# Hot ids as 4 KB spread by TensorE in a recommendation tower, with a new order of the work

## The chip, the core and the metric

The kernel runs on one NeuronCore of a Trainium2 chip. Its engines work side by side and meet through semaphores: TensorE (PE in the profile, with its weight loads as PEld), VectorE (DVE), ScalarE (ACT), GpSimd (POOL) and SyncE (SP), which only issues loads here. The metric is the device time of one execution in microseconds. Before the change it was 199.67 us, the median of three runs (199.2 to 199.85).

## The reference

For 512 samples, 32 tables give one row of 64 numbers each. Every pair of the 32 rows goes through its own 64 x 64 matrix, and the 496 results plus 16 dense features go through three dense layers:

```python
e = jnp.stack([tbl_0[ids[:, 0]], ..., tbl_31[ids[:, 31]]], axis=1)   # (512, 32, 64)
idx_i, idx_j = np.triu_indices(32, k=1)
left = jnp.einsum('bpd,pde->bpe', e[:, idx_i, :], L0_rec_W)
z = jnp.sum(left * e[:, idx_j, :], axis=-1)                          # (512, 496)
h = jnp.concatenate([z, dense_ctx], axis=1)
h = jnp.maximum(h @ W_top1 + b_top1, 0.0)                            # 512
h = jnp.maximum(h @ W_top2 + b_top2, 0.0)                            # 256
y = h @ W_top3
```

Everything is float32, the ids are int32.

## The kernel before

The samples are cut into 4 parts of 128, one sample per partition. The 32 fields form 16 units of two fields. The 496 pairs are covered by 31 groups; group 0 pairs fields inside the units, groups 1 and 2 and the 28 others pair unit with unit. So there are 31 x 4 = 124 group products. For each, TensorE multiplies the turned rows (`xt`) with the pair weights into `left` in PSUM (three slots), and VectorE multiplies `left` with the other fields and writes 1024 numbers per partition. Then the products are summed in one of four ways, the letter in the order: C, TensorE multiplies with a selector (`reduce`, line 737); A, ScalarE adds them by accumulating copies (`add_rows`, line 442, 16 copies each); D, VectorE itself (`sum_rows`, line 611); P, GpSimd by halving (`add_halves`, line 409).

Rows come by indirect DMA on GpSimd (`fetch`, line 396), one field of 128 samples each. "Turning" a unit means transposing it on TensorE (line 692) and copying it to `xt` by ScalarE (an `a` behind the word) or VectorE.

Eight fields with tables of at most 1024 rows are hot. In part 0 their rows, units 12 to 15, are not gathered: the tables are loaded whole, VectorE compares the ids, which lie broadcast over all partitions, with the row numbers (`compare`, line 515, 16 compares), and TensorE multiplies the tables with these 0/1 matrices (`look_up`, line 675). That makes 24 gathers in part 0 and 32 in each of the other parts, 120 in all. The ids of the first 4 hot fields and those of the other 4 each come as a broadcast of 256 KB; their homes are the last `prod_act` buffer.

The order of everything is written by hand in a table of words, `ORDER`. Every engine walks through all of it and takes what is its own, so an engine waits only where its own next step is not ready. In it `o1.0` is a compare (second set, first half), `h1` a look-up, `0g9` a gather (part 0, unit 9), `0t8-11a` a turn of units 8 to 11 by ScalarE, `0:22A` the product of group 22 of part 0, `0=22` its sum, `u` the way back of the hot rows, `f0` and `z0` the end of a part's sums, `l`, `m` and `n` layers 1 to 3. A group of way C reads its other fields from `xt`, so it needs their turn; one of the other ways reads them from `rows`, so it needs their gather.

SyncE loads the ids, the hot ids and the 8 hot tables (256 KB each), then the 31 pair weights (256 KB each). From the ninth on, each of these loads waits until VectorE has taken the product eight places earlier (`W_AHEAD`). Behind them come the dense features and the MLP weights (line 370, 1.5 MB).

Of the kernel before, what the change touches and what calls it, by code (L numbers as in the profile page):

```python
# [11 lines left out]
I32 = mybir.dt.int32  # L12
# [200 lines left out]
def build(nc, a):  # L213
    ctx = ExitStack()
    with ctx:
# [111 lines left out]
        def summed(part, g):  # L327
            way = WAY[part, g]
            return {"A": act_added, "P": pool_summed, "D": dve_summed, "C": reduce_done}[way], SUMS[way].index((part, g)) + 1

        block = ctx.enter_context(nc.Block())

        @block.sync
# [587 lines left out]
```

## Time and profile before

| | |
|---|---|
| median of the runs | 199.67 us |
| time of the profiled execution | 199.53 us |
| its span, first to last instruction | 197.4 us |
| busy: PE, PEld, DVE, ACT, POOL | 189.4, 156.6, 179.8, 170.4, 144.7 us |
| granted TensorE clock, mean | 1.00 |
| moved by DMA | 16.82 MB |

The profile describes the one profiled execution; times inside it are counted from the start of its span. The ends of matmuls are modelled, so a busy PE can be waiting for its next operands or for a free slot; PEld is the safer measure. In the views an fp32 matmul stands as two entries. Neighbouring instructions of VectorE overlap by about 0.08 us, so that the distance of two starts, not the duration, is what one costs.

### The profile page before, as it was taken

How to read it: one execution, taken by the hardware profiler on the slowest of the kernel's cores; microseconds unless marked ns; L12 is line 12 of the kernel's file. 1: busy time of each engine (PE TensorE's matmuls, PEld its weight loads, DVE VectorE, ACT ScalarE, POOL GpSimd, SP SyncE). 2: the span in 40 equal slices, each digit the busy share in tenths (PEclk: the TensorE clock that was granted, in tenths of full speed). 3: DMA queues.
4: the chain of work that ended last, by engine and by line, in shares of the span. 5: the costliest groups of instructions: out<-in, count | busy, mean ns of one | idle time of the engine just before them, and what ended most of it. 6: DMA issues, size and time to landing. Idle time of an engine off the chain costs nothing.

```text
span 197.4 us, 7040 instructions
## 1 busy us (share of the span) xinstructions
PE 189.4 (96%) x2380; PEld 156.6 (79%) x2380; DVE 179.8 (91%) x188; ACT 170.4 (86%) x1535; POOL 144.7 (73%) x181
## 2 busy tenths in 40 slices
PE   6889989899999999999999999999999999999994
PEld 6878848697758688798688878897687788778993
DVE  4656799999989999999999999999999999999951
ACT  6005979799997999999949999999999999999942
POOL 5787777777777777777777777777777997887810
PEclk9999999999999999999999999999999999999999
DMA  4969978867561111111111111111111000000000
GB/s 146 357 226 345 244 216 246 248 211 209 171 213 27 31 27 30 28 30 27 32 29 27 29 28 25 31 27 30 32 27 27 18 2 5 0 0 7 0 0 3
DMA packets 11100, 16.82 MB, mean 85 GB/s; under 512 B 3624, under 2 KB 3624, under 8 KB 10936
## 3 DMA queue, kind: packets, MB, share of 16 engines
q1 hardware_dynamic: 7224, 12.43, 19.1%
q0 software_dynamic: 3840, 3.94, 10.0%
q8 instruction: 19, 0.31, 0.7%
q14 instruction: 17, 0.14, 0.2%
HBM read 16.36 MB, written 0.00 MB: 83 GB/s over the span
## 4 chain that ended last, share of the span: by engine, by line
PE 66%; POOL 18%; issue 7%; DMA 4%; DVE 3%; ACT 0%; DVEq 0%; ACTq 0%; POOLq 0%
PE left L714 26%; POOL rows L396 18%; PE left L724 14%; PE zsum L737 8%; PE left L787 6%; PE left L797 4%; DMA rows<-tbl_dram,ids 3%; PE left L703 3%; PE left L692 2%; PE zsum L745 1%; DVE prod_act L566 1%; PE left L781 1%; PE left L772 1%; DMA ids<-ids_dram 1%; DVE sums L611 1%
## 5 line engine op out<-in xcount | busy, mean ns | idle before, releaser
L442 ACT ACTIVATE prod_act<-prod_act 128x64 f32<-128x64 f32 x752 | 157.7, 588 | 2.5 <-DVE prod_act L566 2.5
L442 ACT ACTIVATION_READ_ACCUMULATOR prod_act<-prod_act 128x1 f32 x752 | 155.5, 501 | 0.0
L396 POOL DMA_INDIRECT rows<-tbl_dram,ids x120 | 114.8, 957 | 37.5 <-issue 32.6
L714 PE MATMUL left<-w,xt 64*128 64x256 f32 (+1 forms) x600 | 72.0, 378 | 1.0 <-DVE prod_act L566 0.9
L714 PEld LDWEIGHTS left<-w,xt 64*128 64x128 f32 x600 | 52.5, 187 | 12.5 <-issue 4.1
L566 DVE TENSOR_TENSOR prod_act<-left,rows 128x1024 f32<-128x1024 f32 x47 | 56.3, 1213 | 5.5 <-PE left L714 3.6
L586 DVE TENSOR_TENSOR prod_col<-left,xt 128x1024 f32<-128x1024 f32 x43 | 50.7, 1214 | 0.7 <-PE left L724 0.2
L724 PEld LDWEIGHTS left<-xt,w 64*128 64x128 f32 x768 | 46.5, 188 | 3.5 <-DVE prod_act L566 1.1
L724 PE MATMUL left<-xt,w 64*128 64x128 f32 x768 | 48.7, 275 | 0.2 <-DVE prod_act L566 0.2
L409 POOL TENSOR_TENSOR prod_pool<-prod_pool 128x512 f32<-128x512 f32 (+4 forms) x45 | 27.3, 608 | 4.9 <-DVE prod_pool L560 1.0
L737 PE MATMUL zsum<-prod_col,selector 128*32 128x256 f32 x384 | 24.6, 384 | 0.0
L611 DVE TENSOR_REDUCE sums<-prod_dve 128x16 f32<-128x1024 f32 x20 | 23.7, 1207 | 0.0
L566 DVE TENSOR_TENSOR prod_dve<-left,rows 128x1024 f32<-128x1024 f32 x16 | 19.2, 1213 | 0.1
L737 PEld LDWEIGHTS zsum<-prod_col,selector 128*32 128x32 f32 x384 | 10.6, 109 | 8.7 <-issue 1.7
L479 ACT ACTIVATE xt<-left 128x512 f32<-128x512 f32 (+5 forms) x12 | 9.1, 771 | 5.7 <-PE left L692 5.7
L787 PE MATMUL left<-z,w 128*128 128x256 f32 (+1 forms) x64 | 12.1, 337 | 0.0
L787 PEld LDWEIGHTS left<-z,w 128*128 128x128 f32 x64 | 9.6, 190 | 2.6 <-DVE prod_act L566 0.8
L471 ACT ACTIVATE xt<-left 128x256 f32<-128x256 f32 x1 | 0.4, 385 | 11.1 <-PE left L675 11.1
L515 DVE TENSOR_SCALAR prod_col<-prod_act,row_cast 128x512 f32<-128x512 int32 x16 | 6.5, 480 | 2.9 <-DMA prod_act<-hot_ids_dram 2.9
L692 PEld LDWEIGHTS left<-ident,rows 64*128 64x128 f32 x120 | 5.2, 138 | 4.5 <-issue 2.3
L703 PE MATMUL left<-w,xt 64*128 64x64 f32 x128 | 7.8, 271 | 0.0
L797 PE MATMUL left<-h,w 128*128 128x128 f32 (+1 forms) x48 | 7.6, 312 | 0.0
(52 smaller groups left out, 110.0 us busy)
## 6 DMA issues: line engine op xcount, KB each, us to landing
w<-pair_w_dram SPq DMA_DIRECT2D x31, 256.0 KB, 3.7
rows<-tbl_dram,ids POOLq DMA_INDIRECT x120, 2.5
w<-tbl_dram SPq DMA_DIRECT2D x6, 256.0 KB, 4.9
w<-w_top_dram SPq DMA_DIRECT2D x1, 1024.0 KB
prod_act<-hot_ids_dram SPq DMA_DIRECT2D x2, 256.0 KB, 4.0
h<-tbl_dram SPq DMA_DIRECT2D x2, 256.0 KB, 6.2
w<-w_top_dram SPq DMA_DIRECT2D x1, 512.0 KB
z<-dense_t_dram SPq DMA_DIRECT2D x16, 2.0 KB
```

Source lines behind the costliest of these rows:

```text
L396: pool.indirect_dma_start(out=rows[:, part % ROW_BUFS, n, h, :], out_offset=None, in_=a[f"tbl_{f}"], in_offset=bass.IndirectOffsetOnAxis(a ...
L409: pool.tensor_tensor(prod[:, :, :half], prod[:, :, :half], prod[:, :, half:2 * half], ALU.add).then_inc(pool_halved, 1)
L442: op = act.activation(p, p, ACT.Copy, accum_out=act_sums[:, k:k + 1])
L566: dve.tensor_tensor(out.rearrange("p (j e) d -> p j (e d)", j=4), slot(item).rearrange("p (j e) -> p j e", j=4), other.unsqueeze(1).to_bro ...
L586: dve.tensor_tensor(out.rearrange("p h (j m) b -> p (h j) (m b)", j=2), slot(item).rearrange("p (j e) -> p j e", j=4), other, ALU.mult).th ...
L611: dve.tensor_reduce(sums_of(part, g), prod.rearrange("p (h u o) d -> p h u o d", h=2, o=2), AXIS.X, ALU.add).then_inc(dve_summed, 1)
L703: mm = pe.matmul(slot(item)[:, col:col + D], xt[own, part % 2, 2 * k + half, :], w[own, INSIDE, :, :].rearrange("p u c -> p (u c)")[:, D * ...
L714: mm = pe.matmul(slot(item)[:, col:col + P * per], xt[own, part % 2, GROUPS[g][i][0], :], w[own, g, i:i + per, :], start=True, stop=True)
L724: mm = pe.matmul(slot(item)[:, col:col + PB], w[own, g, i, :], xt[own, part % 2, n, :], start=True, stop=True)
L737: mm = pe.matmul(zsums(pair)[32 * s:32 * s + 32, :], selector[:, 30 - 2 * q:62 - 2 * q], prod_col[:, (COL_FROM + c) % COL_BUFS, half, odd: ...
L787: mm = pe.matmul(slot(item)[:, :n], w1[:, c, P * k:P * k + P], z[:, c, SPANS[i]], start=(c == 0), stop=(c == NZ - 1))
L797: mm = pe.matmul(slot(item)[:, BANK * o:BANK * o + n], w2[:, k, P * o:P * o + P], h1[:, k, :n], start=(k == 0), stop=(k == H1 // P - 1))
```

## The change

It has two parts. The first is how the hot ids of part 0 reach all partitions. They come as 8 x 128 integers (4 KB) into the first 8 partitions of a `prod_dve` buffer; VectorE casts them to float; for each set of four fields TensorE multiplies them with a column of the identity matrix, broadcast, so that each field's ids appear on all 128 partitions in PSUM (`spread`, in `zsum` and `act_sums`, which are not yet in use); ScalarE copies the 512 numbers to where the loads put them before; VectorE compares floats. The warm-up of TensorE falls from 12 matmuls to 3.

The second is a new `ORDER` for the whole kernel. It has the same 124 products and 120 gathers. 49 groups instead of 48 are summed by TensorE, 47 as before by ScalarE, 20 as before by VectorE, 8 instead of 9 by GpSimd. There are 13 turns instead of 15: 9 by ScalarE (12 before) and 4 by VectorE (3 before).

```diff
--- before.py
+++ after.py
@@ ORDER and ACT_GROUPS @@
-    "o0.0 0g9 0g8 o0.1 0g10 o1.0 o1.1 h0 0g10 0g9 0g11 0g8 h1a 0g11 0g4 0:22A 0g6 0g4 0g6 0g5 0:30C 0t8-11a 0:29C",
...
+    "o0.0 0g9 o0.1 0g7 h0a 0g9 o1.0 o1.1 0g7 0g8 0g6 h1 0g6 0g8 0:21A 0:30C 0g4 0:27D 0:28A 0g5 0=21 0g4 0=30 0g5",
...
-ACT_GROUPS = [15, 19, 24, 11, 18, 22, 9, 8, 20, 23, 21, 6]
+ACT_GROUPS = [21, 23, 10, 28, 26, 29, 25, 14, 0, 8, 18, 6, 16]
@@ -246,7 +246,9 @@
         hot = prod_col[:, :len(HOT_FIELDS)].rearrange("p f h u b -> p f (h u) b")
         id_homes = [prod_act[:, ACT_BUFS - 1, 8 * i:8 * i + 8, :].rearrange("p e d -> p (e d)") for i in (0, 1)]
         id_homes.append(h2.rearrange("p c b -> p (c b)"))
-        hot_ids = [t.bitcast(I32).rearrange("p (f b) -> p f b", b=PB) for t in id_homes]
+        hot_ids = [t.rearrange("p (f b) -> p f b", b=PB) for t in id_homes]
+        id_rows = prod_dve[:len(HOT_FIELDS), 0, :2, :].rearrange("p e d -> p (e d)")
+        id_rows_int = prod_dve[:len(HOT_FIELDS), 1, :2, :].rearrange("p e d -> p (e d)").bitcast(I32)
         whole = [w1[:, i, :] for i in range(4)]
         whole += [t[:, 2 * i:2 * i + 2, :].rearrange("p c b -> p (c b)") for t in (w2, h1) for i in (0, 1)]
         whole += [prod_pool[:, i // 2, 8 * (i % 2):8 * (i % 2) + 8, :].rearrange("p e d -> p (e d)") for i in range(4)]
@@ -258,7 +260,10 @@
 
         ids_loaded = sem("ids_loaded")
         later_ids_loaded = sem("later_ids_loaded")
-        hot_ids_loaded = [sem(f"hot_ids_loaded{d}") for d in range(HOT_SETS)]
+        hot_ids_loaded = sem("hot_ids_loaded")
+        hot_ids_cast = sem("hot_ids_cast")
+        hot_ids_spread = sem("hot_ids_spread")
+        hot_ids_copied = sem("hot_ids_copied")
         tables_loaded = [sem(f"tables_loaded{n}") for n in range(HOT_FROM, NP)]
         row_no_ready = sem("row_no_ready")
         row_cast_ready = sem("row_cast_ready")
@@ -328,6 +333,9 @@
             way = WAY[part, g]
             return {"A": act_added, "P": pool_summed, "D": dve_summed, "C": reduce_done}[way], SUMS[way].index((part, g)) + 1
 
+        def spread_ids(d):
+            return (zsum, act_sums)[d][:]
+
         block = ctx.enter_context(nc.Block())
 
         @block.sync
@@ -340,14 +348,10 @@
             def load_w(g):
                 sp.dma_start(w[:, g, :, :], a["pair_w"][g]).then_inc(w_loaded[g], 16)
 
-            def load_ids(d):
-                sp.dma_start(hot_ids[d], a["hot_ids"][d]).then_inc(hot_ids_loaded[d], 16)
-
             sp.dma_start(ids[:, 0, :], a["ids"][:P, :]).then_inc(ids_loaded, 16)
-            load_ids(0)
+            sp.dma_start(id_rows_int, a["hot_ids"]).then_inc(hot_ids_loaded, 16)
             load_hot(0)
             for d in range(1, HOT_SETS):
-                load_ids(d)
                 load_w(W_ORDER[d - 1])
                 load_hot(d)
             load_w(W_ORDER[HOT_SETS - 1])
@@ -431,6 +435,9 @@
             act.activation(y[:, :1], selector[:, :1], ACT.Copy)
             act.activation(sums[:].rearrange("p t k -> p (t k)"), selector[:, :1].to_broadcast([P, PARTS * NZ * P]), ACT.Copy
                            ).then_inc(sums_zero, 1)
+            for d in range(HOT_SETS):
+                act.wait_ge(hot_ids_spread, d + 1)
+                act.activation(hot_ids[d].rearrange("p f b -> p (f b)"), spread_ids(d), ACT.Copy).then_inc(hot_ids_copied, 1)
 
             def add_rows(part, g):
                 act.wait_ge(*taken(ITEM[part, g])[0])
@@ -497,6 +504,8 @@
             dve.wait_ge(row_no_ready, 1)
             dve.tensor_copy(row_cast[:], row_no[:]).then_inc(row_cast_ready, 1)
             dve.memset(z[:, 2:, :], 0.0).then_inc(dense_zero, 1)
+            dve.wait_ge(hot_ids_loaded, 16)
+            dve.tensor_copy(id_rows, id_rows_int).then_inc(hot_ids_cast, 1)
             dve.wait_ge(row_cast_ready, 1)
             sure = set()
 
@@ -510,7 +519,7 @@
 
             def compare(d, half):
                 if half == 0:
-                    dve.wait_ge(hot_ids_loaded[d], 16)
+                    dve.wait_ge(hot_ids_copied, d + 1)
                 for k in range(HOT_PER // 2 * half, HOT_PER // 2 * half + HOT_PER // 2):
                     dve.tensor_scalar(hot[:, 4 * d:4 * d + 4, k, :], hot_ids[d], row_cast[:, k:k + 1], None, ALU.is_equal
                                       ).then_inc(hot_made, 1)
@@ -660,8 +669,16 @@
         def _(pe):
             def warm_up():
                 pe.wait_ge(ident_ready, 1)
-                for _ in range(12):
+                for _ in range(3):
                     pe.matmul(slot(ITEMS[0])[:, BANK:BANK + P], ident[:], ident[:], start=True, stop=True)
+
+            def spread(d):
+
+                for f in range(4):
+                    mm = pe.matmul(spread_ids(d)[:, PB * f:PB * f + PB],
+                                   ident[:len(HOT_FIELDS), 4 * d + f:4 * d + f + 1].to_broadcast([len(HOT_FIELDS), P]),
+                                   id_rows, start=True, stop=True)
+                mm.then_inc(hot_ids_spread, 1)
 
             def look_up(item):
                 d = item[1]
@@ -810,6 +827,9 @@
                 mm.then_inc(left_done, 1)
 
             warm_up()
+            pe.wait_ge(hot_ids_cast, 1)
+            for d in range(HOT_SETS):
+                spread(d)
             sure = set()
 
             def turned(part, units):
@@ -898,9 +918,7 @@
         tbl[:len(arrays[f"tbl_{f}"])] = arrays[f"tbl_{f}"]
         arrays[f"tbl_{f}"] = tbl
     arrays["ids"] = np.asarray(inputs["ids"])
-
-    hot_ids = arrays["ids"][:PB, HOT_FIELDS].T.reshape(HOT_SETS, 1, 4, PB)
-    arrays["hot_ids"] = np.broadcast_to(hot_ids, (HOT_SETS, P, 4, PB))
+    arrays["hot_ids"] = arrays["ids"][:PB, HOT_FIELDS].T
     arrays["pair_w"] = pair_w
     arrays["dense_t"] = np.asarray(inputs["dense_ctx"]).T
     arrays["w_top1"] = w_top1[row_of]
```

TensorE at the start of the program, before: the warm-up, the look-ups from the tables (their buffers appear as `w` and `h`), then the first products, 714 being ways A, D and P, 724 way C, and 692 the transposes of a turn.

```order
L664 MATMUL left<-ident 128x128 x12
L675 MATMUL left<-prod_col,w 64x128 x48
L675 MATMUL left<-prod_col,h 64x128 x16
L714 MATMUL left<-w,xt 128x256 x4
L724 MATMUL left<-xt,w 128x128 x8
L692 MATMUL left<-ident,rows 128x64 x8
L724 MATMUL left<-xt,w 128x128 x8
```

The same place now; 673 is the warm-up, 678 the spread, 731 and 741 are the old 714 and 724, 700 is the way back of the hot rows, 709 the transposes.

```order
L673 MATMUL left<-ident 128x128 x3
L678 MATMUL zsum<-prod_dve,ident 128x128 x4
L678 MATMUL act_sums<-prod_dve,ident 128x128 x4
L692 MATMUL left<-prod_col,w 64x128 x48
L692 MATMUL left<-prod_col,h 64x128 x16
L731 MATMUL left<-w,xt 128x256 x4
L741 MATMUL left<-xt,w 128x128 x8
L731 MATMUL left<-w,xt 128x256 x8
L754 MATMUL zsum<-prod_col,selector 32x256 x4
L700 MATMUL left<-ident,xt 128x128 x4
L731 MATMUL left<-w,xt 128x256 x4
L709 MATMUL left<-ident,rows 128x64 x12
```

The spreads stand between a shorter warm-up and the look-ups, and the first turn has moved from behind the second product to behind the fifth and has six units (12 matmuls) instead of four.

VectorE around the first product of part 1 that reads gathered rows, before: the fifth row holds 0:25C and 0:14C, the seventh is 1:22A, and 611 is a row sum.

```order
L586 TENSOR_TENSOR prod_col<-left,xt 128x1024
L566 TENSOR_TENSOR prod_dve<-left,rows 128x1024
L566 TENSOR_TENSOR prod_act<-left,rows 128x1024
L611 TENSOR_REDUCE sums<-prod_dve 128x2x4x2
L586 TENSOR_TENSOR prod_col<-left,xt 128x1024 x2
L566 TENSOR_TENSOR prod_dve<-left,rows 128x1024
L566 TENSOR_TENSOR prod_act<-left,rows 128x1024
L611 TENSOR_REDUCE sums<-prod_dve 128x2x4x2 x2
```

Now (575, 592 and 595 are products, 620 row sums, 535 a turned copy); the fifth and sixth rows are 0:1C and 0:9C, the seventh is 1:29A.

```order
L564 TENSOR_TENSOR prod_act<-left,rows 128x1024
L595 TENSOR_TENSOR prod_col<-left,xt 128x1024 x3
L575 TENSOR_TENSOR prod_act<-left,rows 128x1024
L620 TENSOR_REDUCE sums<-prod_dve 128x2x4x2
L592 TENSOR_TENSOR prod_col<-left,xt 128x1024
L595 TENSOR_TENSOR prod_col<-left,xt 128x1024
L575 TENSOR_TENSOR prod_act<-left,rows 128x1024
L620 TENSOR_REDUCE sums<-prod_dve 128x2x4x2
L575 TENSOR_TENSOR prod_act<-left,rows 128x1024
```

1:22A reads units 8 and 9, and needs the 38th gather of the order; 1:29A reads units 10 and 11 and needs the 39th. Both are the 32nd product.

VectorE towards the end, before: 592 are layer-1 results, 598 layer 2, 604 the output.

```order
L592 TENSOR_SCALAR h<-left,b 128x128
L611 TENSOR_REDUCE sums<-prod_dve 128x2x4x2
L566 TENSOR_TENSOR prod_act<-left,rows 128x1024
L560 TENSOR_TENSOR prod_pool<-left,rows 128x1024
L566 TENSOR_TENSOR prod_act<-left,rows 128x1024
L592 TENSOR_SCALAR h<-left,b 128x128
L615 TENSOR_TENSOR z<-zsum,z 128x2x128
L560 TENSOR_TENSOR prod_pool<-left,rows 128x1024
L566 TENSOR_TENSOR prod_dve<-left,rows 128x1024 x2
L611 TENSOR_REDUCE sums<-prod_dve 128x2x4x2
L592 TENSOR_SCALAR h<-left,b 128x128
L611 TENSOR_REDUCE sums<-prod_dve 128x2x4x2
```

Now, with 601 for layer 1, 607 for layer 2 and 613 for the output.

```order
L620 TENSOR_REDUCE sums<-prod_dve 128x2x4x2
L601 TENSOR_SCALAR h<-left,b 128x128
L575 TENSOR_TENSOR prod_act<-left,rows 128x1024
L575 TENSOR_TENSOR prod_pool<-left,rows 128x1024
L575 TENSOR_TENSOR prod_dve<-left,rows 128x1024 x2
L620 TENSOR_REDUCE sums<-prod_dve 128x2x4x2 x2
L607 TENSOR_SCALAR h<-left,b 128x128
L631 COPY z<-zsum 128x2x128
L613 COPY y<-left 128x32
L601 TENSOR_SCALAR h<-left,b 128x128 x2
```

Of the three layer-1 results among the last products and row sums one is left (601), and two now follow behind the copy of `z` that ends the last fold.

## Rows read from the trace of the kernel before

**Rows 1.** The page, part 1: busy us, share of the span, instructions.
```profile
PE 189.4 (96%) x2380; PEld 156.6 (79%) x2380; DVE 179.8 (91%) x188; ACT 170.4 (86%) x1535; POOL 144.7 (73%) x181
```

**Rows 2.** Windows, 60 to 188 us: busy by engine, then clock, DMA share, GB/s.
```profile
60.00:188.00 128.00, 127.95 (x1561) 105.43 (x1562) 127.27 (x124) 123.61 (x1161) 99.71 (x128) 1.00 0.11 22
```

**Rows 3.** Timeline of VectorE: start, us, what, count, idle before and its releaser.
```profile
8.95 3.26 DVE L515 TENSOR_SCALAR prod_col<-prod_act,row_cast 128x512 f32<-128x512 int32 x8 [1.70 <-DMA prod_act<-hot_ids_dram]
...
16.18 1.22 DVE L566 TENSOR_TENSOR prod_act<-left,rows 128x1024 f32<-128x1024 f32 x1 [3.64 <-PE left L714]
...
24.52 1.23 DVE L566 TENSOR_TENSOR prod_act<-left,rows 128x1024 f32<-128x1024 f32 x1 [1.24 <-DMA rows<-tbl_dram,ids]
...
38.65 4.62 DVE L586 TENSOR_TENSOR prod_col<-left,xt 128x1024 f32<-128x1024 f32 x4
...
56.23 1.22 DVE L566 TENSOR_TENSOR prod_act<-left,rows 128x1024 f32<-128x1024 f32 x1 [0.53 <-DMA rows<-tbl_dram,ids]
...
57.37 2.33 DVE L611 TENSOR_REDUCE sums<-prod_dve 128x16 f32<-128x1024 f32 x2
```

**Rows 4.** Waits: who waited for whom, total us, times, longest.
```profile
DVE prod_act L566 <- DMA rows<-tbl_dram,ids: 1.8, 2, 1.2
```

**Rows 5.** The chain that ended last: start, us, what.
```profile
0.74 1.77 DMA ids<-ids_dram
...
50.45 5.66 DMA rows<-tbl_dram,ids
```

**Rows 6.** Timeline of SyncE's queue at the MLP weights.
```profile
50.80 1.30 SPq L370 DMA_DIRECT2D w<-w_top_dram  x3
```

**Rows 7.** Timeline of GpSimd: the gathers 12, 39 and 41.
```profile
17.92 0.95 POOL L396 DMA_INDIRECT rows<-tbl_dram,ids  x1 [0.30 <-issue]
...
51.70 0.94 POOL L396 DMA_INDIRECT rows<-tbl_dram,ids  x1 [0.30 <-issue]
...
54.20 0.94 POOL L396 DMA_INDIRECT rows<-tbl_dram,ids  x1 [0.30 <-issue]
```

**Rows 8.** Timeline of TensorE: warm-up, last look-ups, first product, eight transposes.
```profile
1.52 4.69 PE L664 MATMUL left<-ident 128*128 128x128 f32 x24 [1.52 <-POOL ident L381]
...
13.15 1.92 PE L675 MATMUL left<-prod_col,h 128*64 128x128 f32 x32
...
14.99 1.13 PE L714 MATMUL left<-w,xt 64*128 64x256 f32 x8
...
50.48 0.46 PE L692 MATMUL left<-ident,rows 64*128 64x64 f32 x8
```

**Rows 9.** Groups by shape: count, busy us, mean ns, idle before.
```profile
L737 PE MATMUL zsum<-prod_col,selector 128*32 128x256 f32 x384 | 24.6, 384 | 0.0
...
L479 ACT ACTIVATE xt<-left 128x768 f32<-128x768 f32 x3 | 3.0, 1002 | 3.3 <-PE left L692 3.3
...
L526 DVE COPY xt<-left 128x512 f32<-128x512 f32 x2 | 1.4, 678 | 0.0
...
L526 DVE COPY xt<-left 128x256 f32<-128x256 f32 x1 | 0.4, 411 | 0.0
...
L592 DVE TENSOR_SCALAR h<-left,b 128x256 f32<-128x256 f32 x2 | 1.0, 478 | 0.0
...
L592 DVE TENSOR_SCALAR h<-left,b 128x128 f32<-128x128 f32 x3 | 1.0, 337 | 0.0
...
L484 ACT ACTIVATE h<-left,b 128x256 f32<-128x256 f32 x2 | 1.5, 736 | 0.0
...
L484 ACT ACTIVATE h<-left,b 128x128 f32<-128x128 f32 x5 | 2.2, 474 | 2.0 <-PE left L781 2.0
```

**Rows 10.** TensorE's line 664: duration ns min/median/max, starts.
```profile
L664 PEld LDWEIGHTS left<-ident x24: 192/333/333, 1.5 to 5.8; 128*128 128x128 f32 x24
```

**Rows 11.** Gathers issued from 17 to 25 us, then the 41st: us to landing.
```profile
DMA to landing us min/median/max: 3.7/4.0/4.3
...
DMA to landing us min/median/max: 4.6/4.6/4.6
```

36 rows, old and new, of the table ORDER are left out of this document.

## Prediction

> **What bounds the kernel now.** I read the busy shares first [rows 1]. TensorE shows 96%, but its matmul ends are modelled; its weight loads, 79%, are nearer to its real load. VectorE shows 91%, and from 60 us to 188 us it is busy 127.27 of 128 us [rows 2]. In that stretch nothing but less VectorE work can shorten the kernel. So I looked for VectorE's idle time ahead of it. There are four pieces: the wait for the hot look-ups before the first product, which starts at 16.18 us after 3.64 us idle; 1.24 us at 24.52; 0.53 us at 56.23 [rows 3]; and the tail. The two middle ones are waits for gathered rows, 1.8 us together [rows 4]. The chain that ended last says the same of the second: a gather issued at 50.45 us needed 5.66 us to land [rows 5], beside the 1.5 MB of MLP weights that SyncE issues from 50.80 us [rows 6].
>
> GpSimd issues the gathers one after another, at 17.92 us the 12th, at 51.70 us the 39th [rows 7]: 27 gathers in 33.78 us, 1.25 us each. The change leaves the number at 120 and nearly leaves this pace. My reading is therefore that the first 57 us are paced by gathers and what follows by VectorE's work. An earlier end of the look-ups only counts if neither wait takes it back.
>
> **Part 1, the hot ids.** Before, two broadcast loads of 256 KB bring them; the second set is compared from 8.95 us, 8 compares in 3.26 us, to 12.21 [rows 3]. The last 32 look-up matmul entries run from 13.15 to 15.07 us, and the first product's matmuls start at 14.99 [rows 8]. Now:
> - The ids land. The general id load starts at 0.74 and lands after 1.77 us [rows 5]; the 4 KB load is issued next, some 0.45 us later (three issues of SyncE take 1.30 us [rows 6]), so it lands at about 3.0.
> - The cast on VectorE of 8 x 128: 0.2 (a 128-element VectorE operation takes 0.34 [rows 9]).
> - The first spread on TensorE: 4 matmuls, 8 entries. The warm-up's 24 entries take 4.69 us [rows 8], 0.2 each, so 1.6.
> - The ScalarE copy of 512 elements: a 768-element one takes 1.00 us [rows 9], so 0.7, and about 0.2 of handing over.
>
> Compares can start at 3.0 + 0.2 + 1.6 + 0.2 + 0.7 = 5.7 us. Sixteen of them at 0.41 are 6.5 us, to 12.2, just where they ended before. The second spread and copy lie under the first eight compares. Each new wait holds up little else: behind VectorE's wait for the ids stand only the compares, behind TensorE's wait for the cast the spreads and look-ups, behind ScalarE's waits for the spreads its first turned copy (idle until 15 us before). After the last compare come a few matmuls and the second table pair's 32 entries, 1.92 us [rows 8]: end at about 14.5 instead of 15.07. Before, this end was held by the tables' loads, not by the compares; 0.5 MB less in front of them removes that. The first product starts at about 15.7 rather than 16.18: 0.5 us gained, bounds +0.8 (all steps faster) and -0.6 (the spread's chain a microsecond later). The trace shows no compare of floats. The nearest rows bound it: a 256-wide copy takes 0.33 net of overlap, a 512-wide one out of PSUM 0.60 [rows 9], so sixteen compares change by -1.2 to +3.1 us. I take 0, the row that they are nearest to being today's compare; the upper end would put the first product at 18.8.
>
> The warm-up falls from 12 matmuls to 3. The granted clock reads 1.00 from the start, yet the warm-up's weight loads last 333 ns in the median and 192 ns at their fastest [rows 10], so by their durations they begin at the lower level of 1.2 GHz and end at 2.4. TensorE is then busy but for half a microsecond before the spreads, so I let the look-ups run at 2.4 GHz. If they didn't, the last 32 entries would cost 1.9 us more: the first product at 17.6. The Trainium skill ("TensorE: Matmul & The Clock Gate", Part 1) says that the array starts at half clock, reaches the full one after sustained work and falls back in a pause. By that rule a shorter warm-up and a pause speak against the change. Here the first gate hides it.
>
> **Part 2, the first gate.** Now the fifth product (0:26A) and the turn of units 4 to 9 need the 12th gather. VectorE's sixth product (0:22C) reads what this turn writes. Gather 12 is issued at 17.92; gathers of 17 to 25 us land after 3.7 to 4.3 us, median 4.0 [rows 11]: 21.9. Then 20 transposes are left (8 in 0.46 us [rows 8]), 1.1, and ScalarE's 768-element copy, 1.0, with 0.2 of handing over: 0:22C starts at 24.2, bounds 23.6 and 24.8. VectorE's work ahead of it is five products and one row sum. One product costs 1.13 us, from (4.62 - 0.08)/4 [rows 3] as neighbours overlap by 0.08; a row sum 1.13 as well (two in 2.33). With 6.8 us of work, a first product anywhere up to 17.4 us is hidden; 18.8 would show 1.4 here, and the second gate would take that back but for 0.1. Before, after the same 6.8 us of work, VectorE stood at 24.52. The gain is 0.3 us, whatever the look-ups do.
>
> **Part 3, the second gate.** Between here and the first product of part 1 that reads gathered rows (1:22A before, 1:29A now) lie 26 products, one row sum and two turned copies: 29.5 + 1.1 + 0.33 + 0.60 = 31.5 us (the copies by [rows 9]). VectorE would arrive at 24.2 + 31.5 = 55.7, with small gaps 55.9. But 1:29A needs the 39th gather (second half of unit 10) where 1:22A needed the 38th. The 38th landed at 50.45 + 5.66 = 56.11. The 41st, issued at 54.20, took 4.6 us: 58.8 [rows 11]. Evenly spaced, the 39th lands at 57.0. The MLP weights are issued once the 23rd product is taken and all loads before are out; that point moves by +0.2 at most. So 1:29A starts at 57.0, where 1:22A started at 56.23: 0.8 us later. Bounds: 55.9 (the gate is open) and 58.3 (just ahead of the 41st).
>
> **Part 4, work after the second gate.** On both sides 93 products and 18 row sums follow, and two 512-element turned copies. What differs is layer 1: before, VectorE took two 256-wide and three 128-wide results ahead of the last fold; now one and one. At 0.40 and 0.26 us (0.478 and 0.337 less the overlap [rows 9]) that is 0.40 + 0.52 = 0.92 us less. They go to ScalarE, which is busy 123.61 of 128 us [rows 2] and has the same 47 row groups; three more results of 0.5 to 0.7 us [rows 9] fit in its 4.4 us, and it makes nine turned copies instead of twelve. GpSimd has eight groups instead of nine. TensorE gets one more column group: 24.6 us over 48 of them [rows 9] is 0.5 us, covered by weight loads at 82% of that stretch. In the tail two more results go to VectorE where it is idle: 0.
>
> **Sum.** +0.77 at the second gate, -0.92 behind it: -0.15. From the profiled execution, span 197.4 and time 199.53, this gives 199.4; the runs' median is 199.67, so the profiled one is typical.
>
> **Rivals.**
> - A, the second gate opens early. The 0.5 MB are gone, and a gather need not queue behind the MLP weights. For it: uncongested gathers land faster, and the 38th may have been the unlucky one, issued 0.35 us before the weights. Against: the 41st still took 4.6 us. Then 1:29A starts at 55.9, -0.33 - 0.92 = -1.25: 198.3. The Trainium skill ("DMA: Bandwidth & Descriptors", Queues, rings and completion order) says that a DMA engine alternates between its queues packet by packet. By that rule the 39th gather would overtake most of the 1.5 MB, and this rival holds.
> - B, slower: the second gate closes harder. The 39th gather, issued at 51.70 with the weights already flowing, is served just ahead of the 41st, at 58.3: +2.07 - 0.92 = +1.15, so 200.7. It decides from a landing of 57.15, where the sum is zero; measurably slower from 57.8.
> - C, the new order has a wait of its own after 60 us, most likely behind the single eight-unit turns of part 3 (ScalarE copies of over 1.00 us behind 32 transposes of 1.8 us) or TensorE's extra group. Before, that stretch shows only 0.73 us of idle [rows 2], so there is little to win and something to lose: +1, so 200.4.
> - D, the look-up chain takes more than 1.7 us longer than I say (cold TensorE and a slow copy together). Then it shows at the first gate; +0.5 there is still absorbed by the second: as the forecast.
>
> **Chances.** Forecast with D 0.45, A 0.27, B 0.16, C 0.12. A measurement here tells about 0.3% (0.6 us) from no change. Faster by more than that needs A, or a second gate at 56.5 or earlier: 0.33. Slower needs most of B or C: 0.24. Within: 0.43. Range: from A's 198.3 to near B's 200.7.
>
> **What would show it.** The profile after should have: compares starting at 5.7 and ending at 12.2 without the pause of before; the first product near 15.7; 0:22C near 24.2 after an idle VectorE; 1:29A near 57.0 after a wait for gathered rows; VectorE over 127 us busy in 60 to 188. A landing of the 39th gather before 56 proves A; waits later than 60 us prove C. Compares much shorter or longer than 0.41 would make Part 1 wrong without moving the end.

## The result and the profile after

The changed kernel took 202.55 us, the median of six runs (201.5 to 203.82), beside 199.49 us for the kernel before. The ratio is 1.0139, with a 95% interval from 1.0092 to 1.0187: slower by 1.4%. Ten more runs later, on a chip that also ran the kernel before, gave 200.55 us (199.19 to 202.4) and a ratio of 1.0045 [0.9998, 1.0092]. The first measurement is clear of noise, the second just touches no change. So I take the kernel as slower, by one to three microseconds, and what it costs changes from run to run. The ratios leave out single runs that took over 1.5% more than the fastest of the same kernel; the medians do not. The profiled run is the slowest of the first six: 203.82 us, span 202.0.

Part 1 of the page, beside [rows 1]:

```profile
PE 191.7 (95%) x2362; PEld 158.8 (79%) x2362; DVE 180.3 (89%) x189; ACT 171.2 (85%) x1535; POOL 144.0 (71%) x175
```

VectorE is busy for about as long, 180.3 us instead of 179.8, in a span that is 4.6 us longer. Its timeline, beside [rows 3]:

```profile
5.92 6.63 DVE L524 TENSOR_SCALAR prod_col<-prod_act,row_cast 128x512 f32<-128x512 f32 x16 [3.02 <-ACT prod_act L440]
...
17.44 1.23 DVE L575 TENSOR_TENSOR prod_act<-left,rows 128x1024 f32<-128x1024 f32 x1 [1.68 <-DMA rows<-tbl_dram,ids]
...
24.87 1.23 DVE L575 TENSOR_TENSOR prod_act<-left,rows 128x1024 f32<-128x1024 f32 x1 [1.68 <-DMA rows<-tbl_dram,ids]
...
60.62 1.23 DVE L575 TENSOR_TENSOR prod_act<-left,rows 128x1024 f32<-128x1024 f32 x1 [2.55 <-DMA rows<-tbl_dram,ids]
...
66.04 1.23 DVE L575 TENSOR_TENSOR prod_act<-left,rows 128x1024 f32<-128x1024 f32 x1 [0.68 <-PE left L731]
...
67.70 2.36 DVE L595 TENSOR_TENSOR prod_col<-left,xt 128x1024 f32<-128x1024 f32 x2 [0.44 <-PE left L741]
```

These rows give the steps. The compares start at 5.92 (5.7 was forecast) and end at 12.55. The first product starts at 17.44 and not at 15.7: it waits 1.68 us for rows. The fifth waits as long for the 12th gather, at 24.87. 1:29A starts at 60.62 after 2.55 us; I had put it at 57.0. GpSimd's timeline says why, beside [rows 7]:

```profile
8.22 4.45 POOL L400 DMA_INDIRECT rows<-tbl_dram,ids  x1 [0.30 <-issue]
...
20.47 0.94 POOL L400 DMA_INDIRECT rows<-tbl_dram,ids  x1 [0.30 <-issue]
...
54.18 0.95 POOL L400 DMA_INDIRECT rows<-tbl_dram,ids  x1 [0.30 <-issue]
```

The fifth gather takes 4.45 us where a free one takes 0.94, and it ends at 12.67, just behind the last compare. The 12th is thus issued at 20.47 instead of 17.92, and the 39th at 54.18 instead of 51.70. The MLP weights leave at 53.11, beside [rows 6]:

```profile
53.11 1.31 SPq L374 DMA_DIRECT2D w<-w_top_dram  x3
```

So the 39th gather is issued a microsecond behind them, and the product that waits for it starts 6.4 us later. Meanwhile TensorE has nothing to do (the timeline):

```profile
58.30 2.37 PE L754 MATMUL zsum<-prod_col,selector 128*32 128x256 f32 x40
...
63.11 0.68 PE L762 MATMUL zsum<-ident,sums 128*128 128x128 f32 x4 [2.44 <-DVE sums L620]
```

Its last sum entry ends at 60.67, and the fold f0 at 63.11 needs VectorE's row sum, which stands in the queue behind 1:29A. Busy time by stretch, with the columns of [rows 2]:

```profile
60.00:63.00 3.00, 0.67 (x15) 0.13 (x4) 2.38 (x3) 1.12 (x11) 2.09 (x4) 1.00 0.12 23
64.00:67.00 3.00, 3.00 (x27) 2.70 (x24) 2.32 (x5) 3.00 (x33) 2.22 (x3) 0.51 0.10 22
60.00:188.00 128.00, 125.24 (x1513) 102.10 (x1504) 125.38 (x120) 122.11 (x1132) 94.79 (x118) 0.99 0.11 22
```

The granted clock is 1.00 up to this pause and 0.51 from 64 to 67 us, the lower of the two levels. With TensorE at 1.2 GHz, VectorE waits for it twice, 0.68 and 0.44 us (at 66.04 and 67.70). Both kernels now divide at the start of the 32nd product, 60.62 against 56.23 us: +4.39. From there to the end of the span it takes 141.2 us before and 141.4 now. In the profiles of the new order below whose granted clock stays up (e2 to e5, e7 to e9) it takes 139.9, so the new order itself saves 1.3 us here, and the fall of the clock costs 1.5: the two waits of 1.12 us, and smaller ones that I did not add up. Together +4.39 - 1.3 + 1.5 = +4.6, and the span grew by 4.6.

The look-ups on TensorE differ as well. In the kernel before, 64 of their entries take 3.71 us; now 96 take 6.73, and 7.65 with the old order (e1 below):

```profile
6.84 3.71 PE L675 MATMUL left<-prod_col,w 128*64 128x128 f32 x64 [0.63 <-DMA w<-tbl_dram]
```

```profile
6.81 6.73 PE L692 MATMUL left<-prod_col,w 128*64 128x128 f32 x96
```

```profile
6.83 7.65 PE L692 MATMUL left<-prod_col,w 128*64 128x128 f32 x96
```

That is 58, 70 and 80 ns each. Between 7 and 9 us one of their weight loads lasts 230 ns in the changed kernel and 137 ns in the kernel before. The granted clock reads 1.00 in both, as it did for the warm-up; by the durations, the new look-ups begin at the lower level.

### The profile page after: what moved, and what is told of

Read it like the earlier page. It is cut to its first block, busy times and chain, and to the rows that moved or that the text cites. A ratio compares the mean times of both kernels' runs of the same rounds, so it can differ in the third digit from the quotient of the medians.

```text
span 202.0 us, 6993 instructions
## 1 busy us (share of the span) xinstructions
PE 191.7 (95%) x2362; PEld 158.8 (79%) x2362; DVE 180.3 (89%) x189; ACT 171.2 (85%) x1535; POOL 144.0 (71%) x175
## 4 chain that ended last, share of the span: by engine, by line
PE 67%; DVE 8%; issue 8%; POOL 7%; ACT 6%; DMA 3%; DVEq 0%; ACTq 0%
PE left L731 26%; PE left L741 15%; PE zsum L754 8%; POOL rows L400 7%; PE left L804 6%; ACT prod_act L449 5%; PE left L814 4%; DVE prod_col L595 3%; PE left L720 3%; DMA rows<-tbl_dram,ids 2%; DVE prod_act L575 2%; PE left L709 2%; PE zsum L762 2%; DVE sums L620 1%; PE left L798 1%
## 5 line engine op out<-in xcount | busy, mean ns | idle before, releaser
L400 POOL DMA_INDIRECT rows<-tbl_dram,ids x120 | 117.3, 977 | 37.3 <-issue 32.6
L731 PE MATMUL left<-w,xt 64*128 64x256 f32 x568 | 72.9, 391 | 0.7 <-DVE prod_act L575 0.6
L575 DVE TENSOR_TENSOR prod_act<-left,rows 128x1024 f32<-128x1024 f32 x43 | 51.6, 1219 | 6.7 <-DMA rows<-tbl_dram,ids 5.9
L595 DVE TENSOR_TENSOR prod_col<-left,xt 128x1024 f32<-128x1024 f32 x41 | 48.5, 1217 | 0.8 <-PE left L741 0.7
L413 POOL TENSOR_TENSOR prod_pool<-prod_pool 128x512 f32<-128x512 f32 (+4 forms) x40 | 24.3, 608 | 10.2 <-DVE prod_pool L575 7.7
L575 DVE TENSOR_TENSOR prod_dve<-left,rows 128x1024 f32<-128x1024 f32 x20 | 23.8, 1217 | 0.0
L486 ACT ACTIVATE xt<-left 128x512 f32<-128x512 f32 (+2 forms) x9 | 7.8, 868 | 4.9 <-PE left L709 4.7
L575 DVE TENSOR_TENSOR prod_pool<-left,rows 128x1024 f32<-128x1024 f32 x8 | 9.7, 1220 | 0.6 <-PE left L731 0.5
L592 DVE TENSOR_TENSOR prod_col<-left,xt 128x1024 f32<-128x1024 f32 x8 | 9.7, 1218 | 0.0
L524 DVE TENSOR_SCALAR prod_col<-prod_act,row_cast 128x512 f32<-128x512 f32 x16 | 6.6, 491 | 3.0 <-ACT prod_act L440 3.0
L709 PE MATMUL left<-ident,rows 64*128 64x64 f32 x120 | 6.5, 230 | 2.3 <-DMA rows<-tbl_dram,ids 2.3
```

The costliest lines, as they stand in the source:

```text
L400: pool.indirect_dma_start(out=rows[:, part % ROW_BUFS, n, h, :], out_offset=None, in_=a[f"tbl_{f}"], in_offset=bass.IndirectOffsetOnAxis(a ...
L413: pool.tensor_tensor(prod[:, :, :half], prod[:, :, :half], prod[:, :, half:2 * half], ALU.add).then_inc(pool_halved, 1)
L575: dve.tensor_tensor(out.rearrange("p (j e) d -> p j (e d)", j=4), slot(item).rearrange("p (j e) -> p j e", j=4), other.unsqueeze(1).to_bro ...
L592: dve.tensor_tensor(out, slot(item).rearrange("p (h u b) -> p h u b", h=2, b=PB), other, ALU.mult).then_inc(dve_taken, 1)
L595: dve.tensor_tensor(out.rearrange("p h (j m) b -> p (h j) (m b)", j=2), slot(item).rearrange("p (j e) -> p j e", j=4), other, ALU.mult).th ...
L709: mm = pe.transpose(slot(item)[:, BANK * half + D * i:BANK * half + D * i + D], rows[own, part % ROW_BUFS, n + i, :, :].rearrange("p h d - ...
```

## The experiments

My theory after the result, S with G and K: VectorE's compares, which read and write SBUF, keep GpSimd from finishing gathers (S); the second gate is the gather queueing beside the MLP weights (G); the pause there costs the clock as well (K). The rivals were that the order itself is what costs (O), that the gather's late issue is all (P), that floats matter (F), and that the wait counts but not the clock (W). All ratios are to the kernel before on the same chip.

| kernel | order | hot ids | MLP weights | median us (runs) | ratio [95%] | runs with mean clock under 0.995 | longest gather, us |
|---|---|---|---|---|---|---|---|
| before, on four chips | old | old | early | 199.20 to 199.54 (99) | 1 | 17 | 1.28 |
| e1 | old | new | early | 199.31 (10) | 1.0001 [0.9960, 1.0043] | 0 | 1.28 |
| e2 | new | old | early | 200.81 (10) | 1.0075 [1.0036, 1.0114] | 7 | 1.67 |
| e9 (the change) | new | new | early | 200.55 (10) | 1.0045 [0.9998, 1.0092] | 5 | 2.86 |
| e6 | old | old | late | 199.43 (10) | 0.9976 [0.9948, 1.0004] | 1 | 1.68 |
| e11 | old | new | late | 199.39 (10) | 0.9995 [0.9957, 1.0033] | 0 | 2.47 |
| e7 | new | old | late | 197.52 (5) | 0.9894 [0.9857, 0.9932] | 0 | 1.28 |
| e5 | new | new | late | 199.6 (10) | 1.0006 [0.9979, 1.0033] | 1 | 4.05 |

The kernel before has runs with a fallen clock too, 17 of 99; they have medians of 201.1 to 201.5 us on the four chips, its other runs 199.2 to 199.5. The new order has them more often, in 7 of 10 (e2, and again e10) and 9 of 16 runs (the change). No profile caught such a run of the old order, so where it loses its clock is not known.

**e1, the new hot ids alone.**

```diff
-ORDER = [ "o0.0 0g9 o0.1 0g7 h0a ...   # the new table
+ORDER = [ "o0.0 0g9 0g8 o0.1 0g10 ...  # the table of before
```

> The hot ids of the change (4 KB, cast, spread, ScalarE copy, float compares, 3 warm-up matmuls) with the order of before. Theory S (16 compares without a pause keep GpSimd from writing its gathers): one gather takes over 4 us again, the gathers behind it are 2.5 us late, both gates of the order before (0:11A at 24.5, 1:22A at 56.2) move by about 2.5, and the time is about 2 to 2.5 us over before. Rival O (the new order is what costs): gates where they were, time equal to before within 0.5 us.

The time is that of before. The compares run without a pause, from 5.94 us, yet the gathers behind them look like this:

```profile
8.26 1.28 POOL L400 DMA_INDIRECT rows<-tbl_dram,ids  x1 [0.30 <-issue]
...
9.85 1.28 POOL L400 DMA_INDIRECT rows<-tbl_dram,ids  x1 [0.30 <-issue]
```

So an unbroken row of compares does not have to block a gather for long. Theory S as I wrote it fell; O gained. The first product starts at 17.34 us, 1.2 later than in the kernel before, after a wait of 4.13 us for TensorE and none for rows: here it is the slow look-ups that hold it. The waits of the old order for rows hide that, and 1:22A starts at 55.83.

**e2, the new order alone.** (The kernel before with the new table.)

> The new order with the hot ids of before (two broadcast loads, int32 compares, 12 warm-up matmuls). Theory S: there is a pause between the two sets of compares, no gather takes over 1.3 us, the 39th gather is issued near 51.7 and 1:29A starts near 57: time as I had forecast, within 0.5 us of before. Rival O: 1:29A near 60 and 2 to 3 us over before.

```profile
11.35 1.67 POOL L396 DMA_INDIRECT rows<-tbl_dram,ids  x1 [0.30 <-issue]
...
52.10 0.95 POOL L396 DMA_INDIRECT rows<-tbl_dram,ids  x1 [0.30 <-issue]
```

```profile
57.80 1.22 DVE L566 TENSOR_TENSOR prod_act<-left,rows 128x1024 f32<-128x1024 f32 x1 [2.14 <-DMA rows<-tbl_dram,ids]
```

No gather is blocked for long, and the order still costs 1.5 us. The 39th is issued at 52.10, 0.4 later than in the kernel before, and lands 5.7 us later, so the gate opens at 57.80, after a wait of 2.14 us. I expected 57 and 0.5 us at most; the gate alone is enough to make the order slower, in seven runs of ten with a fall of the clock. VectorE does not wait at the first gate: 0:22C starts at 23.70, 6.8 us of work behind the first product.

**e3, a gap between the compares.**

```diff
+                    if d == 1:
+                        for b, lo, hi in ((0, 4, 12), (1, 4, 12), (0, 12, 16), (1, 12, 16)):
+                            dve.tensor_copy(prod_dve[:, b, lo:hi, :]..., spread_ids(0)[:, :D * (hi - lo)])
```

> The changed kernel with four copies from PSUM on VectorE (1536 elements, about 1.9 us of work whose result nobody reads) between the two sets of compares. They use one SBUF port. Theory S: the long gather ends when the first set ends, near 9.3 us instead of 12.7, later gathers are 2.5 us earlier, 1:29A starts near 57 to 58 and the time falls by about 2.5 us, although VectorE does more work and the first product comes no earlier. Rival: gathers late for another reason (DMA rings full of early weight loads): no gather moves, time the same or up to 1 us longer.

199.96 us, ratio 1.0029 [0.9996, 1.0062]. The 12th gather is issued at 18.60 and 1:29A starts at 58.75, earlier than in the first profile of the changed kernel, though VectorE has more work. But the second profile of the changed kernel (e9) has 1:29A at 58.70, and the time is 2.6 us under the first measurement of the change and only 0.6 under the second. One gather in the second set still took 2.07 us. So this run does not decide about S.

**e4, compares straight from PSUM.**

```diff
-                    dve.wait_ge(hot_ids_copied, d + 1)
+                    dve.wait_ge(hot_ids_spread, d + 1)
-                    dve.tensor_scalar(hot[...], hot_ids[d], ...
+                    dve.tensor_scalar(hot[...], spread_ids(d).rearrange("p (f b) -> p f b", b=PB), ...
```

> The changed kernel with compares that read the spread ids straight from PSUM; ScalarE's copies are gone. Each compare then takes about 0.6 us instead of 0.41, so sixteen take 9.6 us from 5.1 to 14.7, and the first product starts near 18.3. Theory S: with one PSUM source VectorE leaves the shared port alone, no gather is longer than 1.3 us, the 12th is issued at 17.9 or earlier, 0:22C starts near 25 and 1:29A near 57: 2 to 3 us under the changed kernel. Rival (back-to-back VectorE work of any kind starves GpSimd): one gather takes over 4 us again and the time rises by 1 to 2 us.

GpSimd's timeline in the midst of the compares, then VectorE's:

```profile
9.17 0.94 POOL L400 DMA_INDIRECT rows<-tbl_dram,ids  x1 [0.30 <-issue]
...
10.42 0.94 POOL L400 DMA_INDIRECT rows<-tbl_dram,ids  x1 [0.30 <-issue]
```

```profile
5.29 5.36 DVE L521 TENSOR_SCALAR prod_col<-zsum,row_cast 128x512 f32<-128x512 f32 x8 [2.39 <-PE zsum L675]
...
10.56 5.35 DVE L521 TENSOR_SCALAR prod_col<-act_sums,row_cast 128x512 f32<-128x512 f32 x8
...
19.27 1.22 DVE L572 TENSOR_TENSOR prod_act<-left,rows 128x1024 f32<-128x1024 f32 x1 [0.64 <-PE left L728]
...
57.93 1.21 DVE L572 TENSOR_TENSOR prod_act<-left,rows 128x1024 f32<-128x1024 f32 x1
```

Every gather beside the compares takes 0.94 or 0.95 us, although VectorE is busy without a break, and the time is 199.64 us, ratio 1.0003 [0.9972, 1.0034]. So what lengthens the gathers is compares that have both their input and their output in SBUF; e8 shows the same inside one kernel.

The first product starts at 19.27, 3.1 us later than in the kernel before, and from there to 1:29A VectorE waits for nothing. This start is not free: 1:29A comes at 57.93, 1.7 us later than the 32nd product of the kernel before. What e4 gains is the second gate, in a way that I had not foreseen. The MLP weights are issued once the 23rd product is taken, so they come later too, in SyncE's queue:

```profile
53.08 1.30 SPq L374 DMA_DIRECT2D w<-w_top_dram  x3
```

The 39th gather, issued at 50.37, is 2.7 us ahead of them and lands after 2.9 us. The second gate is a race between this gather and these weights.

All ten runs lie between 199.63 and 199.66, where ten of the changed kernel spread over 3.2 us. That the scatter comes from the compares in SBUF is likely but not shown by e4 alone, since it also waits for no gather anywhere. e8 waits for none either, in its profile, compares from SBUF in its second set, and spreads over 2.2 us. The Trainium skill ("SBUF — State Buffer", SBUF: two separate sides) has this as a trap: an SBUF port pair is shared by VectorE and GpSimd as an exclusive lock, and while VectorE holds it GpSimd cannot write the descriptors of the DMAs that it issues. The runs agree: 0.94 us from PSUM, and from SBUF usually 1.28, which is 0.34 us or most of one compare (0.41 us) more, but up to 4.45. Why a gather is sometimes held for many compares in a row, no trace shows.

**e9 and e10, the change again, and with int32 compares.** For e10 ScalarE writes the spread ids as int32:

```diff
-        hot_ids = [t.rearrange("p (f b) -> p f b", b=PB) for t in id_homes]
+        hot_ids = [t.bitcast(I32).rearrange("p (f b) -> p f b", b=PB) for t in id_homes]
```

> The changed kernel again, for a second profile. If its blocked gather is its rule, one gather of the first seven again takes over 3 us and the 39th is issued near 54; the time is 202 to 203. If it is a matter of chance, the gathers may all be under 1.7 us, and the profiled time is then near e2's 200.8.

> The changed kernel with the ids written as int32 by ScalarE, and int32 compares as before. Theory F (float compares block GpSimd, int32 ones less): no gather over 1.7 us, time near e2's 200.8. Rival C (it is the sixteen compares without a pause, whatever their type): a gather of 4 us again in this order, time near the changed kernel's 202.5.

Both profiles have one gather of 2.86 us. e9 thus falls between its two forecasts: its 39th gather is issued at 52.78, behind weights at 51.45, and 1:29A starts at 58.70:

```profile
58.70 1.23 DVE L575 TENSOR_TENSOR prod_act<-left,rows 128x1024 f32<-128x1024 f32 x1 [2.29 <-DMA rows<-tbl_dram,ids]
```

Its first product starts at 17.66 and waits for TensorE, not for rows; TensorE pauses ahead of f0 for 2.27 us, and its granted clock stays at 1.00. e10 took 201.5 us, ratio 1.0088 [1.0046, 1.0130]. F fell: with int32 the gather is held as long. Over the seven profiles with sixteen compares in a row from SBUF (e12 included) the longest gather took 4.45, 4.05, 2.86, 2.86, 2.86, 2.47 and 1.28 us; over the five with a pause or other work between the sets 2.07, 1.68, 1.67, 1.28 and 1.28. The lack of a pause makes a long block likelier and not certain.

**e5, e6, e7, e11, late MLP weights.**

```diff
+            for t in taken(ITEM[MAINS[44]]):
+                sp.wait_ge(*t)
             for dst, name in ((w1, "w_top1"), (w2, "w_top2"), ...
```

> The changed kernel, but SyncE issues the MLP weights (1.5 MB) only once the 45th product is taken, near 75 us. Theory G (the second gate is the gather queueing beside these weights): the 39th gather lands 2.5 us after its issue, 1:29A starts without a wait at about 58, TensorE doesn't stand idle there and its clock keeps the upper level, and the time falls by 2.5 to 3.5 us to about 199.5. Rival P (the gather is late because GpSimd issues it late): it is issued as late as before and the gate stays near 60, time down by less than 0.7.

> The kernel before with the MLP weights held back in the same way. Theory G: its wait of 0.53 us at 56.2 goes, time down by 0.5 us to about 198.8. Rival P: no change.

> The new order with the hot ids of before (e2) and late MLP weights. Theory G: the 2.14 us wait at 57.8 goes, 1:29A starts at 55.7 to 56, and with 0.9 us less VectorE work behind it the time is about 198.2, under both kernels, and its runs scatter less. Rival P: as e2, 200.8.

> The order before with the new hot ids (e1) and late MLP weights: the last of the eight combinations. The old order has only 0.5 us behind the second gate to give, and its first gate stays: 199.0 to 199.3, the same as before within 0.3%. If late MLP weights by themselves were worth something in any order, it would come near e7's 197.5.

In e5 the fifth gather is blocked again, for 4.05 us, but 1:29A starts as soon as VectorE gets there:

```profile
57.65 1.22 DVE L577 TENSOR_TENSOR prod_act<-left,rows 128x1024 f32<-128x1024 f32 x1
```

The time falls to 199.6 us. In e7 the order works as it should; the 38th gather, issued at 50.38 us, takes 2.5 us to land, and 1:29A has no wait:

```profile
DMA to landing us min/median/max: 2.5/2.5/2.5
```

```profile
55.59 1.21 DVE L568 TENSOR_TENSOR prod_act<-left,rows 128x1024 f32<-128x1024 f32 x1
```

e7 takes 197.52 us: 1.1% faster than the kernel before and clearly faster than the changed one. It is the best of all. G holds. P fell for the second gate, but the late gathers are not free: e5 and e7 differ only in the hot ids, and e5 is 2.1 us slower. Its 1:29A starts 2.06 us later, after a first product at 17.25 instead of 16.92 and a wait of 1.55 us at the first gate. The old order gains nothing measurable (e6, where I had expected 0.5 us, and e11), since its wait was 0.53 us, and the first gate stays.

**e8, the first set from PSUM and late weights.**

> The changed kernel with late MLP weights, and the first set of compares read from PSUM (8 of 0.67 us, from 5.3 to 10.7), the second from SBUF as now (3.3 us, to 14.0). The shared port is in use for half as long, and the first product starts near 17 us. Theory S with G: hardly a gather over 1.3 us, the first gate near 24, no second gate, time about 198.3 with runs closer together than the changed kernel's. Rival (the start of the products counts): the products start no earlier than in e4, so the time stays near 199.6.

198.88 us, ratio 0.9961 [0.9930, 0.9992]. Beside the first set, from PSUM, every gather takes 0.94 us; beside the second, from SBUF, two take 1.25 and 1.19. The first product starts at 18.27 rather than 17, and no gate holds. Below before, though 0.6 us above what I expected, and not as good as e7: its first product is 1.35 us later than e7's and its 1:29A 1.36 us later. With both gates open the start of the products counts in full.

**e12, TensorE kept busy at the gate.**

```diff
+                    if step[1] == 0:
+                        ...
+                        for _ in range(10):
+                            pe.matmul(slot(after)[:, :P], ident[:], ident[:], start=True, stop=True)
                     fold(step[1])
```

> The changed kernel with ten idle matmuls (20 entries, 2.1 us, results unread) on TensorE just ahead of the fold f0, where it otherwise stands idle for over 2 us while VectorE waits for the 39th gather. The gathers and the gate stay as they are. Theory K (what makes the change slower than its work says is TensorE's clock falling to the lower level after this pause): no run has a mean clock under 0.995 any more, the runs over 201 us vanish, and the median is near 199.7, though a few tenths of extra TensorE work are in it. Rival W (the wait at the gate itself costs, the clock little): the median stays between 200.5 and 202.5.

TensorE's timeline (852 are the added ones); VectorE's gate is at 58.75 after 2.40 us:

```profile
58.79 2.50 PE L852 MATMUL left<-ident 128*128 128x128 f32 x20
...
61.25 0.68 PE L762 MATMUL zsum<-ident,sums 128*128 128x128 f32 x4
```

None of the twelve runs has a mean clock under 0.995, against nine of the changed kernel's sixteen. So in the new order the pause is what lets the clock fall, though it does not always (e9). But the median is 200.7 us, ratio 1.0054 [1.0025, 1.0083], within what rival W had expected: K was right on the clock and wrong on the time. In e9 the five runs without a fall have a median of 199.79 us, the five with one 201.77.

The profiles say what a fall costs. From the start of 1:29A to the end of the span it takes 139.9 us in e12, as in e9 without a fall, and 141.4 and 141.3 in the two profiles with one (the changed kernel and e10). So the fall costs 1.4 to 1.5 us, and the extra matmuls give that back at no cost of their own. That the median of e12 is nevertheless e9's must then lie in the start of 1:29A, which varies from run to run. By an estimate, the spans less 139.9 us, or less 141.35 with a fall, this start lies between 57.4 and 60.7 us over the sixteen runs of the changed kernel. The median is 58.8, and 58.9 in e12's runs; in e9's ten alone it is 58.05. Only a profile shows the start itself, so this stays an estimate.

## Why the prediction was wrong

- **The reading was half right.** VectorE's work sets what follows 57 us. But gathers pace what is ahead of it only through their waits. In e7, with no long gather and the weights out of the way, VectorE works from its first product at 16.92 to 1:29A at 55.59 without a wait, and in e4 and e8 a later first product moves 1:29A by as much.
- **Part 1, the hot ids**, was right in its times: compares at 5.92 (5.7 forecast) to 12.55, 6.6 us as before. Its conclusion, a first product at 15.7, was wrong for two reasons. In the profiled run rows were missing. In e1 and e9 they were there, and it still started at 17.34 and 17.66, because the look-ups ran at TensorE's lower level until about 9 to 12 us. I had let them run at 2.4 GHz and priced the other case for the last 32 entries only, which ran at full pace; it was the first 96 that took 1.1 to 2.4 us more than at 58 ns each. Rival D named the cold TensorE. The two spreads took 2.07 and 1.91 us instead of 1.6 each. With the old ids the new order starts at 16.9 (e2, e7). In no profile do the new hot ids start the products earlier.
- **"Nearly leaves this pace" is one step that failed.** I saw the compares only as VectorE's time, and weighed no rule on the port that VectorE shares with GpSimd. The kernel before already shows it in rows that I had not put to use: its gathers take up to 1.28 us beside compares and 0.94 later. By moving the compares together the change made a block of up to 4.45 us possible, and everything that GpSimd issues later moves by it, 2.5 us in the profiled run.
- **Part 2, the first gate**, was about right in size and mostly did not matter: 0:22C at 24.2 forecast; with the 12th gather 2.5 us late, 26.32. With the gathers on time it starts at 23.7 without a wait (e2, e7). In e7 1:29A starts at 55.59, where I had forecast 55.9 for an open gate.
- **Part 3, the second gate, is the step that decided.** I spaced the landings between the 38th and the 41st and took 57.0 us. With the gathers nearly on time it is 57.80 (e2), in the two profiles of the change 58.70 and 60.62: issued behind the weights, the 39th takes 5.7 to 6.4 us. I also held the weights' issue fixed to 0.2 us, where it moves with VectorE: 50.73 in e2, 53.11 in the profiled run, and 53.08 in e4, where the gather got ahead and the gate was open. Rival B had the mechanism, with 58.3 us, 200.7 us and a chance of 0.16; that is e9's size and too small for the first six runs. Rival A, by which the gather would have overtaken the weights, as the Trainium skill's rule on alternating queues ("DMA: Bandwidth & Descriptors", Queues, rings and completion order) made me think, is refuted by the same numbers: behind 1.5 MB this gather took 5.7 us or more, and 2.5 to 2.9 without it (e5, e8, e11).
- **What hung on the wait, no step had.** The fold needs the row sum behind 1:29A, TensorE pauses for 2.4 us, and its granted clock falls from 1.00 to 0.51. In the profile of the order before the same gate makes no such pause. The fall is worth 1.5 us in the profiled run. I had thought of TensorE's clock at the start only, and not at this place.
- **Part 4** had the right sign: -0.92 forecast, and -1.3 in every profile of the new order without a fall. What makes the other 0.4 I did not trace. C was wrong: VectorE waits once for about 0.5 us near 166 us, and the stretch still takes less time than before.

With early weights the ids alone cost nothing measurable (e1), the order alone 1.5 us (e2), and both together 0.9 to 2.8 us by the two ratios. Whether they are then worse together than the order alone is not settled. With late weights it is: the order alone gains 1.1% (e7, 0.9894 [0.9857, 0.9932]), and with the new ids that is gone (e5, 1.0006 [0.9979, 1.0033]). So the order was the good half of the change, once the weights are held back, and the new ids the bad one.

## What to carry to other kernels

Find the resource that issues late work in order, here GpSimd's gathers, and ask of a moved instruction what it does to that one, not only what it costs its own engine. A wait of half a microsecond in a profile can be the edge of something larger: see what large loads start just ahead of it, and hold back those that nobody needs soon. Then look at what stands in the queues behind the waiting instruction, because an idle TensorE can pay a second time with its clock.

## What the runs showed of the hardware

- VectorE compares with input and output in SBUF lengthen GpSimd's indirect gathers from 0.94 to mostly 1.28 us, and now and then one of them to between 1.67 and 4.45 (after, e2, e3, e5, e6, e9 to e12). With the input in PSUM they don't (e4), at 0.67 instead of 0.41 us per compare.
- With that contention gone and no wait for a gather left, ten runs scattered by 0.03 us (e4) instead of 3.2 (e9).
- The 39th gather, 32 KB, took 5.7 to 6.4 us when issued behind 1.5 MB of direct loads, and 2.9 us when issued 2.7 us ahead of them (e4).
- After a pause of 2.4 us TensorE's granted clock was about 0.5 for 3 us, which cost 1.4 to 1.5 us (after, e10). After one of 2.27 us it stayed at 1.00 (e9).
